# Conv-capsule and attention kernel on one Trainium2 core: the attention loop's body holds four units in place of two

## The chip, the core and the metric

The program runs on one core of a Trainium2 chip. A core has a matrix engine (TensorE, PE in the profile, with its weight loads shown apart as PEld), a vector engine (VectorE, DVE), a scalar engine (ScalarE, ACT), GpSimd (POOL) and SyncE (SP), which here only issues DMA transfers. Each engine has a sequencer of its own that walks through that engine's instructions; engines meet through semaphores. The metric is device time in microseconds (us) for the whole program. Time before: 13452.97 us, the median of three runs (13446.22 to 13472.08).

## The reference

Input x is 16 x 32 x 64 x 64, float32. Layer 0 adds a convolutional capsule layer with three routing rounds to x, layer 1 adds an attention block over 3x3 patches. The change touches only the attention of layer 1:

```
t = patches of the group-normed x          # per sample 4096 tokens x 288
z = _ln2(t)                                # normed over the whole sample
qkv = (z @ Wr.T) @ Wqkv.T                  # 8 heads of 18, tokens in 4 chunks of 1024
attn = softmax(q @ k.T * 18 ** -0.5)       # 1024 x 1024 within a chunk and a head
t = t + concat_heads(attn @ v) @ Wp.T + bp
t = t + relu(_ln2(t) @ W1.T + b1) @ W2.T + b2
out = fold of t back to the image (overlapping patches summed)
```

## The kernel before

The program is five phases, one after the other, with a barrier between them: a group norm (`norm_phase`), the capsule routing (`routing_phase`), a second norm that also prepares the layer norm, attention (`attention_phase`), and the MLP with the fold (`fold_phase`). In the profiled execution the attention phase takes the time from about 4550 to 12680 us.

A unit of attention is one chunk of one sample: 16 samples x 4 chunks make 64 units, numbered 0 to 63, of 1024 tokens each. `unit(p, which)` is written once for each engine; p holds the unit's number n, its parity h (which of two buffers) and m = n // 2, each a Python number or, in the loop, an expression of the loop's register. `which` says which neighbours' work is done beside unit n: 0 is the unit itself, 1 the row maxima for the next unit, 2 the projections and the staging through DRAM for the one after, -1 the remains of the one before. In a unit TensorE goes through 32 steps of four pairs. A pair is one score matmul (L1325, `a_sc`) and one matmul for the maxima of the next unit (L1337, `a_mp`). VectorE reduces each `a_mp` (L1503), ScalarE takes the exponential of each `a_sc` (L1423, 128 of them in a unit), and TensorE multiplies these with the values (L1351, `a_po`). `TASKS` puts the remaining work of a unit (projection, transposes, output) at fixed steps; "qk" of step 6 (L1269) reads the window `a_zw` that SyncE loads at the unit's start (L1138).

SyncE's part of a unit is `unit` at L1188: wait for the values' matmuls and load the window for unit n+2 (L1192), store and reload the row maxima (L1194), load patches (L1198), store results, write q and k parts to DRAM and read them back as stacks (L1215 and L1223). The last of these, 12 transfers of 144 KB (L1161), are issued when the last score of the unit is made.

`run_units` (L980) writes the same sequence for all engines: units -2 to 1 in straight code, a loop (`engine.Fori`, one for each engine, with a compare and branch at the end of its body that L986 marks in the profile), then units 62 to 64 in straight code. The loop runs 30 times over two units, 2 to 61 in all. Between two units of one body no branch stands; the 30th branch of an engine isn't taken. There is no barrier in the loop: engines hold each other only by semaphores. Order within an engine is as written; no scheduler changes it.

Of the kernel before, what the change touches and what calls it, by code (L numbers as in the profile page):

```python
# [979 lines left out]
def run_units(engine, units, unit):  # L980


    for n, which in ((-2, (2,)), (-1, (1, 2)), (0, (0, 1, 2)), (1, (-1, 0, 1, 2))):
        unit(Pass(n, n % 2, n // 2), which)
    if units > 4:
        with engine.Fori(0, units // 2 - 2) as i:  # L986
            unit(Pass(2 * i + 2, 0, i + 1), (-1, 0, 1, 2))
            unit(Pass(2 * i + 3, 1, i + 1), (-1, 0, 1, 2))
    for n, which in ((units - 2, (-1, 0, 1)), (units - 1, (-1, 0)), (units, (-1,))):
        unit(Pass(n, n % 2, n // 2), which)  # L990

# [8 lines left out]
def attention_phase(nc, ctx, sems, halves, ln_halves, mixed, moments, w_r, w_qkv, w_p, consts):  # L1000
# [126 lines left out]
    def _(sp):  # L1127
# [60 lines left out]
        def unit(p, which):  # L1188
# [31 lines left out]
            if 2 in which:  # L1220
                if 0 in which:
                    sp.wait_ge(score_made.sem, score_made.at(p.n, QUAD * STEPS))
                load_stack(offset(p, 2), 1)  # L1223

        run_units(sp, units, unit)
        for stored in t1_stored:
            sp.wait_ge(stored.sem, stored.at(units, 0))
# [3 lines left out]
    @block.gpsimd  # L1231
    def _(pool):
        def unit(p, which):
            for t in sorted(TASKS):
                d, kind, k = TASKS[t]
                if d in which and kind == "qk":
                    n = offset(p, d).n
                    pool.wait_ge(second.sem, second.at(n, k + 1))
                    nc.gpsimd.tensor_tensor(piece(k, 2), left[:, k % 2, 0:width(k)], piece(k, 1),  # L1239
                                            ALU.subtract).then_inc(third.sem, 1)  # L1240

        run_units(pool, units, unit)

    @block.tensor
    def _(pe):
# [110 lines left out]
        def unit(p, which):  # L1356
            for t in range(STEPS):
# [9 lines left out]
                task(p, t, which)  # L1367

        run_units(pe, units, unit)

    @block.scalar
# [533 lines left out]
```

## Time and profile before

| | |
|---|---|
| median of three runs | 13452.97 us |
| profiled execution, its own time | 13459.34 us |
| its span, first to last instruction | 13457.6 us |
| mean granted TensorE clock | 0.969 |
| TensorE busy (matmul) | 12585.8 us, 94% |
| VectorE busy | 9717.1 us, 72% |
| ScalarE busy | 7873.1 us, 59% |
| GpSimd busy | 2684.5 us, 20% |

The span is the profiled execution's own time less the 1.7 us around it. Busy shares are of the whole span. Matmul ends are modelled, so TensorE reads busier than it is. An idle time that is put down to "issue" is one in which the engine waited for nothing that the profile shows. Register, branch and semaphore instructions aren't counted as busy; they carry a q behind the engine's name (ACTq). In the profile FUSED_REGOPS is what the program's order calls ISA, ALU_OP is REGISTER_ALU.

### The profile page before, as it was taken

What the parts mean: (1) busy time and instruction counts of PE and PEld (TensorE: products, weight loads), DVE (VectorE), ACT (ScalarE), POOL (GpSimd) and SP (SyncE); (2) the same over time, 40 slices, a digit from 0 to 9 for tenths busy, and PEclk for the clock granted to TensorE, in tenths of its full rate; (3) what the DMA queues carried; (4) which work ended last, traced back from release to release, by engine and by line L of the source; (5) the groups of instructions that cost most, each with busy time, mean ns of one, the idle gap of its engine ahead of it and who ended that gap; (6) DMA issues with size and microseconds to landing.
All of it is one profiled execution on the core that took longest, in us unless ns stands there. A gap on an engine that the chain in (4) does not pass through costs nothing. (4 is left out here: it accounts for less than half of the span.)

```text
span 13457.6 us, 258672 instructions
## 1 busy us (share of the span) xinstructions
PE 12585.8 (94%) x76348; PEld 5302.5 (39%) x76348; DVE 9717.1 (72%) x18034; ACT 7873.1 (59%) x14774; POOL 2684.5 (20%) x2692
## 2 busy tenths in 40 slices
PE   6999999999996599999999999999999999999899
PEld 3554454554443133333333333333333333333233
DVE  7888888888887577777777777777777777777411
ACT  4666666666665266666666666666666666666511
POOL 3444454444443000000000000000000000000144
PEclk9999999999998699999999999999999999999999
DMA  3101101011012432232332332232232232232354
GB/s 75 22 15 22 22 15 22 15 22 21 16 22 76 107 72 62 69 68 62 70 67 62 70 67 62 69 68 62 69 68 62 69 69 62 68 69 62 73 121 106
DMA packets 853449, 773.62 MB, mean 57 GB/s; under 512 B 587076, under 2 KB 621348, under 8 KB 840740
## 3 DMA queue, kind: packets, MB, share of 16 engines
q1 hardware_dynamic: 850468, 747.29, 24.6%
q8 instruction: 744, 12.19, 0.4%
q10 hardware_dynamic: 1536, 8.39, 0.3%
q14 instruction: 701, 5.74, 0.2%
HBM read 510.50 MB, written 244.96 MB: 56 GB/s over the span
## 5 line engine op out<-in xcount | busy, mean ns | idle before, releaser
L1503 DVE TENSOR_REDUCE a_big<-a_mp 128x1 f32<-128x512 f32 x8192 | 5230.6, 685 | 2109.0 <-PE a_mp L1337 1978.0
L1423 ACT ACTIVATE a_ex<-a_sc 128x512 f32<-128x512 f32 x8192 | 4430.5, 600 | 2227.1 <-PE a_sc L1325 1918.1
L1325 PE MATMUL a_sc<-a_qs,a_ks 111*128 111x512 bf16 x8192 | 3166.8, 388 | 227.0 <-ACT a_ex L1423 152.2
L1337 PE MATMUL a_mp<-a_ks,a_qs 108*128 108x512 bf16 x8192 | 3173.2, 388 | 32.6 <-DMA a_ks<-qk_parts 25.1
L849 DVE TENSOR_TENSOR r_prod<-r_pg,r_win 128x512 f32<-128x512 f32 x3584 | 2317.0, 682 | 528.3 <-PE r_pg L583 287.6
L1351 PE MATMUL a_po<-a_ex,a_va 128*32 128x512 f32 x16384 | 2208.3, 611 | 1.4 <-ACT a_oc L1429 0.7
L1325 PEld LDWEIGHTS a_sc<-a_qs,a_ks 111*128 111x128 bf16 x8192 | 802.2, 98 | 2750.6 <-ACT a_ex L1423 1902.3
L1239 POOL TENSOR_TENSOR a_pieces<-a_left,a_pieces 128x512 bf16<-128x512 f32 x256 | 295.5, 1154 | 7622.9 <-ACT a_pieces L1409 7622.9
L524 POOL TENSOR_TENSOR r_prod<-r_temp,r_win 128x512 f32<-128x512 f32 x1024 | 1215.1, 1207 | 1394.7 <-PE r_pl L632 594.0
L587 PE MATMUL r_pg<-r_ident,r_spread 128*128 128x128 f32 x9216 | 1194.9, 278 | 112.0 <-DVE r_prod L849 93.4
L587 PEld LDWEIGHTS r_pg<-r_ident,r_spread 128*128 128x128 f32 x9216 | 1004.0, 142 | 567.5 <-DVE r_prod L849 266.1
L1337 PEld LDWEIGHTS a_mp<-a_ks,a_qs 108*128 108x128 bf16 x8192 | 810.6, 99 | 888.0 <-DVE a_big L1503 192.2
L582 PE MATMUL r_pg<-r_stack,r_wv 96*128 96x512 bf16 x2304 | 895.7, 389 | 73.1 <-DVE r_prod L849 55.9
L807 ACT ACTIVATE r_spread<-r_low 128x2048 f32<-128x2048 f32 x512 | 952.0, 1916 | 0.0
L583 PE MATMUL r_pg<-r_stack,r_wv 128*128 128x512 bf16 x2304 | 891.1, 387 | 0.0
L1269 PE MATMUL a_pm<-a_zw,a_wc 96*128 96x512 f32 x1536 | 716.4, 603 | 15.2 <-DVE a_left L1473 13.9
L1351 PEld LDWEIGHTS a_po<-a_ex,a_va 128*32 128x32 f32 x16384 | 324.3, 108 | 849.4 <-ACT a_ex L1423 690.8
L629 PE MATMUL r_ps<-r_prod,r_ws 128*32 128x512 f32 x4096 | 551.4, 611 | 26.0 <-DVE r_prod L849 18.1
L1808 DVE TENSOR_TENSOR f_u<-f_pw,f_three 96x512 f32<-96x512 f32 x128 | 87.8, 686 | 652.9 <-PE f_pw L1677 652.9
L790 ACT COPY r_temp<-r_pg 128x512 f32<-128x512 f32 x1024 | 544.5, 583 | 20.6 <-ACT r_out_t L775 20.6
L632 PE MATMUL r_pl<-r_prod,r_pick 128*32 128x512 f32 x4096 | 549.3, 608 | 4.9 <-DVE r_prod L849 0.5
L582 PEld LDWEIGHTS r_pg<-r_stack,r_wv 96*128 96x128 bf16 x2304 | 226.7, 98 | 692.7 <-DVE r_prod L849 323.1
(192 smaller groups left out, 11673.6 us busy)
## 6 DMA issues: line engine op xcount, KB each, us to landing
a_qs<-qk_parts SPq DMA_DIRECT2D x768, 144.0 KB
a_ks<-qk_parts SPq DMA_DIRECT2D x768, 144.0 KB
qk_parts<-a_pieces SPq DMA_DIRECT2D x128, 768.0 KB, 4.9
f_t<-mixed SPq DMA_DIRECT2D x48, 1536.0 KB, 16.5
a_tw<-second SPq DMA_DIRECT2D x512, 128.0 KB, 3.1
mixed<-a_t SPq DMA_DIRECT2D x256, 256.0 KB, 2.1
r_win<-first SPq DMA_DIRECT2D x128, 280.5 KB, 5.3
a_zw<-layered SPq DMA_DIRECT2D x192, 144.0 KB, 11.4
```

The lines of the kernel that those rows point to most:

```text
L524: nc.gpsimd.tensor_tensor(prod[:, g, :].rearrange("p (a b) -> p a b", b=IMG), temp[:, rank, :].rearrange("p (a b) -> p a b", b=IMG), tap_a ...
L582: pe.matmul(bank[:, :], wv_0[0:96, w], stack[0:96, lane, :], start=True, stop=False)
L583: last = pe.matmul(bank[:, :], wv_12[:, w], stack[:, lane, :], start=False, stop=True)
L587: last = pe.transpose(bank[:, 128 * b:128 * b + 128], spread[:, lane, 16 * kk:16 * kk + 16, :].rearrange("p a b -> p (a b)"), ident[:, :])
L807: nc.scalar.activation(to[:, :, half, :], src[:, :, half].unsqueeze(3).to_broadcast([128, BLK, 64, CLEN]), ACT.Exp).then_inc(prob[r].sem, 1)
L849: nc.vector.tensor_tensor(prod[:, g, :].rearrange("p (a b) -> p a b", b=IMG), pg[use % RINGS][:, :].rearrange("p (a b) -> p a b", b=IMG), ...
L1269: last = pe.matmul(pm[:, :], wc[:, i, 128 * (k % WIDE):128 * (k % WIDE) + 128], zw[:, own.h, first:first + CHUNK], start=i == 0, stop=i == 2)
L1325: pe.matmul(sc[k % BANKS][:, :], ks[0:KROWS + NPART, p.h, head, 128 * kb:128 * kb + 128], qs[0:KROWS + NPART, p.h, head, CHUNK * qb:CHUNK ...
L1337: pe.matmul(mp[k % BANKS][:, :], qs[0:KROWS, p.h, head, 128 * q:128 * q + 128], ks[0:KROWS, p.h, head, CHUNK * half:CHUNK * half + CHUNK], ...
L1351: last = pe.matmul(po[32 * x:32 * x + 32, :], va[:, p.h, kb, QUAD * quad + x, :], ex[:, (QUAD * t + x) % RING, :], start=kb == 0, stop=kb ...
L1423: nc.scalar.activation(ex[:, k % RING, :], sc[k % BANKS][:, :], ACT.Exp, scale=scale).then_inc(exped.sem, 1)
L1503: nc.vector.tensor_reduce(big[:, x % 2, k // 2:k // 2 + 1], mp[k % BANKS][:, :], AX_X, ALU.max).then_inc(maxed.sem, 1)
```

## The change

The loop's body is written for four units; the loop runs 15 times. The units' numbers, their order and the code before and after the loop are as they were. Unit k of the body has parity k % 2 and m = 2i + 1 + k // 2, the values that it had.

```diff
     if units > 4:
-        with engine.Fori(0, units // 2 - 2) as i:
-            unit(Pass(2 * i + 2, 0, i + 1), (-1, 0, 1, 2))
-            unit(Pass(2 * i + 3, 1, i + 1), (-1, 0, 1, 2))
+        with engine.Fori(0, (units - 4) // 4) as i:
+            for k in range(4):
+                unit(Pass(4 * i + 2 + k, k % 2, 2 * i + 1 + k // 2), (-1, 0, 1, 2))
```

ScalarE's order at the end of the second unit of a body, before the change: its last exponentials, and the loop's branch.

```order
1510 L1420 REGISTER_ALU
1511 L1423 ACTIVATE a_ex<-a_sc 128x512
1512 L1420 REGISTER_ALU
1513 L1423 ACTIVATE a_ex<-a_sc 128x512
1514 L986 REGISTER_ALU
1515 L986 COMPARE_AND_BRANCH
```

The same place with the change:

```order
1510 L1420 REGISTER_ALU
1511 L1423 ACTIVATE a_ex<-a_sc 128x512
1512 L1420 REGISTER_ALU
1513 L1423 ACTIVATE a_ex<-a_sc 128x512
1514 L1420 ISA
1515 L1422 REGISTER_ALU
1516 L1423 ACTIVATE a_ex<-a_sc 128x512
```

The branch has gone from here (it now stands at row 2174), and the third unit's exponentials follow at once. ScalarE's body grows from 672 to 1331 rows, its head stays at row 845.

SyncE's order at the same place (`a_qs` and `a_ks` are the stacks, `a_zw` the window), before:

```order
437 L1161 DMA a_qs<-qk_parts 18x4x1024
438 L1161 DMA a_ks<-qk_parts 18x4x1024
439 L986 REGISTER_ALU
440 L986 COMPARE_AND_BRANCH
```

and with the change:

```order
437 L1161 DMA a_qs<-qk_parts 18x4x1024
438 L1161 DMA a_ks<-qk_parts 18x4x1024
439 L1191 ISA
440 L1138 ISA
441 L1138 DMA a_zw<-layered 32x18x64
442 L1138 ISA
```

The window load of the next unit follows without a branch; SyncE's branch stands at row 615, and its body has 363 rows where it had 188. On TensorE and VectorE the branch goes from the same place in the same way (rows 3306 and 2014 before, 4487 and 2634 now), on GpSimd the body grows from 22 to 42 rows.

## Rows read from the trace of the kernel before

**Rows 1.** The page: an engine's busy us, share of the span, instructions

```profile
PE 12585.8 (94%) x76348; PEld 5302.5 (39%) x76348; DVE 9717.1 (72%) x18034; ACT 7873.1 (59%) x14774; POOL 2684.5 (20%) x2692
```

**Rows 2.** Busy time by stretch; columns are in the first line

```profile
core 0: us, PE busy (x) PEld busy (x) DVE busy (x) ACT busy (x) POOL busy (x), PEclk, DMA share, GB/s
4650.00:5128.00 478.00, 477.65 (x2644) 180.95 (x2644) 365.21 (x651) 312.81 (x617) 21.15 (x20) 0.99 0.27 64
5142.00:5146.00 4.00, 3.21 (x9) 1.25 (x9) 1.71 (x3) 3.71 (x8) 0.00 (x0) 0.50 0.68 140
5146.00:5380.00 234.00, 233.96 (x1305) 89.44 (x1307) 175.91 (x314) 151.27 (x299) 10.58 (x10) 1.00 0.27 63
```

**Rows 3.** L986, whole run: operation, count; ns min/median/max; first and last start

```profile
L986 PEldq ALU_OP  x30: 32/32/32, 5129.1 to 12455.2; - x30
L986 PEldq COMPARE_BRANCH  x30: 83/3662/3930, 5129.2 to 12455.3; - x30
...
L986 ACTq COMPARE_BRANCH  x30: 40/45/59, 5130.5 to 12456.5; - x30
...
L986 DVEq COMPARE_BRANCH  x30: 55/63/74, 5132.3 to 12458.4; - x30
...
L986 PEldq MOVE  x1: 34/34/34, 4887.3 to 4887.3; - x1
```

**Rows 4.** L986, from 5128 to 5140 us: the first branch of each engine

```profile
L986 ACTq COMPARE_BRANCH  x1: 59/59/59, 5130.5 to 5130.5; - x1
...
L986 DVEq COMPARE_BRANCH  x1: 74/74/74, 5132.3 to 5132.3; - x1
...
L986 ACTq FUSED_REGOPS  x1: 73/73/73, 5134.4 to 5134.4; - x1
...
L986 SPq COMPARE_BRANCH  x1: 50/50/50, 5136.8 to 5136.8; - x1
L986 SPq FUSED_REGOPS  x1: 68/68/68, 5137.1 to 5137.1; - x1
L986 DVEq FUSED_REGOPS  x1: 85/85/85, 5138.0 to 5138.0; - x1
```

**Rows 5.** Timeline of ACT and PE, same boundary: start, us, instruction, [idle before <-releaser]

```profile
5142.14 2.07 ACT L1423 ACTIVATE a_ex<-a_sc 128x512 f32<-128x512 f32 x4 [11.13 <-issue]
...
5142.79 0.61 PE L1325 MATMUL a_sc<-a_qs,a_ks 111*128 111x512 bf16 x1 [6.08 <-ACT a_ex L1423]
```

**Rows 6.** Timeline of ACT, boundary inside a body

```profile
5263.32 1.68 ACT L1423 ACTIVATE a_ex<-a_sc 128x512 f32<-128x512 f32 x3 [0.76 <-PE a_sc L1325]
```

**Rows 7.** Timeline of ACT, 5890 to 5902, boundary with a branch

```profile
5899.97 2.06 ACT L1423 ACTIVATE a_ex<-a_sc 128x512 f32<-128x512 f32 x4 [8.97 <-issue]
```

**Rows 8.** Timeline of ACT, 11190 to 11202, boundary with a branch

```profile
11200.48 2.07 ACT L1423 ACTIVATE a_ex<-a_sc 128x512 f32<-128x512 f32 x4 [8.78 <-issue]
```

**Rows 9.** Timeline of ACT, 12213 to 12216, last branch that is taken

```profile
12214.38 2.06 ACT L1423 ACTIVATE a_ex<-a_sc 128x512 f32<-128x512 f32 x4 [10.16 <-issue]
```

**Rows 10.** L1423, whole run: what ended ACT's idle time; us, times

```profile
  issue: 308.0, 60
```

**Rows 11.** L317, the routing loop's branch, 744 to 760 us

```profile
L317 ACTq COMPARE_BRANCH  x1: 45/45/45, 752.5 to 752.5; - x1
...
L317 ACTq FUSED_REGOPS  x1: 59/59/59, 754.9 to 754.9; - x1
```

**Rows 12.** The window load L1138, 5137 to 5260 us

```profile
L1138 SPq DMA_DIRECT2D a_zw<-layered x3: 332/789/3787, 5137.4 to 5138.9; - x3
...
DMA to landing us min/median/max: 8.0/10.4/10.7
```

**Rows 13.** Its reader L1269, same stretch

```profile
L1269 PEld LDWEIGHTS a_pm<-a_zw,a_wc x24: 187/190/192, 5168.1 to 5192.9; 96*128 96x128 f32 x24
```

**Rows 14.** The page, DMA queues of instruction code: packets, MB, share

```profile
q8 instruction: 744, 12.19, 0.4%
...
q14 instruction: 701, 5.74, 0.2%
```

## The prediction

> **What bounds the kernel now.** I read the page's busy times first. TensorE is busy 94% of the span [rows 1], and in straight attention code all of it: 477.65 of 478.00 us between 4650 and 5128 [rows 2]. So inside a unit TensorE sets the pace, and this change gives TensorE no less to do: matmuls, exponentials, reductions and transfers are the same in number and order. What can move is the code between units, so I went to the loop's own line, L986.
>
> There the branch itself is seen. On ScalarE and VectorE it takes 45 and 63 ns, on TensorE 3662 ns in the median, and only 83 ns where it isn't taken (the minimum, the last of 30) [rows 3]. ScalarE's and VectorE's branches are short but what follows is not. At the first loop end ScalarE branches at 5130.5 and the body's first instruction runs at 5134.4, 3.9 us later; VectorE goes from 5132.3 to 5138.0, 5.7 us; SyncE from 5136.8 to 5137.1, 0.3 us [rows 4]. A sequencer that jumps back to a body it has long passed must get that code again, and waits for it; SyncE's short body was still at hand. The timeline then shows the whole price. ScalarE's first exponential comes at 5142.14, after 11.13 us idle with nothing that released it, and TensorE, which had got going, waits 6.08 us for ScalarE [rows 5]. ScalarE is therefore the engine whose restart ends last. Its head runs three instructions (front order: the head at row 845) and then waits a second time, 5134.4 to 5142.1, which I take for a second piece of code that has to come. After that TensorE runs at a granted clock of 0.50 for about 4 us, 1.2 GHz in place of 2.4, and is back at 1.00 in the next stretch [rows 2]; its matmul takes 0.61 us there [rows 5]. What it did before was to stand idle for 6 us.
>
> At a boundary inside a body nothing of this is seen: the exponential at 5263.32 starts after 0.76 us of an ordinary wait for its score, and the next unit's follow it without a gap [rows 6]. So one back branch costs some ten microseconds on the path, and I have 29 of them that are taken.
>
> **The change part by part.** Price of one taken branch, three ways. (a) Whole iterations: TensorE's branch goes from 5129.1 to 12455.2 in 29 iterations, 7326.1 / 29 = 252.6 us each; the first iteration, which is entered from straight code, takes 4887.3 to 5129.1, 241.8 us [rows 3]. The difference is 10.8 us, and holds the low clock too. (b) The last taken branch: ScalarE stands 10.16 us [rows 9] and its loop ends at 12456.5 [rows 3], 242.1 us after it restarts at 12214.4; with the half microsecond from a branch to the next exponential that is 242.6, so 252.6 - 242.6 = 10.0 us. (c) All the idle time of ScalarE before L1423 that nothing released is 308.0 us in 60 times [rows 10]; even if all of it were these 29, it is 10.6 each. I take 10.3, the middle of (a) and (b).
>
> Removed: 30 iterations have 29 taken branches, 15 have 14. 15 x 10.3 = 154.5 us. The idle times are not equal: of the 29, seven are short ones of 8.2 to 9.0 us, the first at 5899.97 with 8.97, the last at 11200.48 with 8.78 [rows 7, 8], the others 10.2 to 11.9. From unit 12 on the short ones come before every eighth unit (12, 20, 28, ...). The new loop ends stand before units 6, 10, 14, ... 58, so if the short ones belong to the unit, six of the seven are among the removed, and the removed 15 are worth 0.5 us less each than the mean, 147 us in all. If they belong to the count of loop ends, nothing is lost. I can't tell which, and take half: 154.5 - 4 = 150 us.
>
> Kept: the 14 branches that remain. Nothing before the loop changes and the body's head is the same on each engine, so the jump lands at the same place of the code, and ScalarE should wait twice as now. The branch's distance grows, but on TensorE, VectorE and ScalarE the head was already gone. I cost this at zero change, with bounds 2.2 us either way per branch (the difference between a short and a long idle time), 31 us over 14.
>
> New boundaries: 15 places where the third unit follows the second without a branch. The order rows show ScalarE with one ISA and one register operation where branch and head stood. A boundary of that parity is seen in the straight code before the loop, which runs four units without a branch at 0.99 of the clock [rows 2]. Cost zero; the cover is that TensorE has matmuls queued.
>
> SyncE: its body grows from 188 to 363 rows. Now it does not wait at its branch. ScalarE's routing loop of 459 rows (131 to 590 in the order) does, from 752.5 to 754.9, 2.4 us [rows 11]. 363 lies between the two, nearer to the one that waits, so I expect SyncE to wait 2.4 us or more at the 14 branches. Queued behind is the window load L1138, then the row maxima's store. Now the last window transfer starts at 5138.9 and lands at the latest 10.7 us later, 5149.6 [rows 12]; its reader on TensorE starts at 5168.1 [rows 13]. 18.5 us of slack hide 2.4 us, and also the 11.6 us that ScalarE's restart takes (5130.5 to 5142.1). The store after it is for scores half a unit, 60 us, later. What SyncE can cost is its fetch standing in the way of ScalarE's second one: between nothing and 3.9 us, ScalarE's first wait [rows 4], on 14 branches, 0 to 55 us; or a gain, since the window load then leaves the queues free while ScalarE's code comes, up to the 2.2 us above. The nearest row is the loop end as it is, so I take zero and keep both ends.
>
> GpSimd's body grows from 22 to 42 rows; it works 10 instructions in two units and waits for others. Zero. The fold loop behind lies at another place of the code; its bodies are short, and I cost it at zero.
>
> Sum against the profiled execution: span 13457.6 - 150 = 13308, its own time 13459.3 - 150 = 13309. The median of the runs is 6.4 us below the profiled one, so the forecast is 13453 - 150 = 13303 us, 1.1% less.
>
> **Where the Trainium skill is weighed.** The trace shows 3662 ns for TensorE's branch and 10 us for the whole stop. The Trainium skill, Advanced Engine Details and Errata, Control Flow Timing, gives about 108 ns for a compare-and-branch; by that figure alone 15 of them would be worth 1.6 us and the change would do nothing. For the branch on ScalarE and VectorE the trace is below that figure (45 and 63 ns), for what follows it is not. The Trainium skill, Runtime: NRT & Kernel Launch, Instruction fetch mechanics, says that a taken branch to code outside the small window of instruction memory stalls for a fetch, and that straight code is fetched ahead. By this rule rows 4 and 6 are what one should see, and the sum is the one above. The same section gives the window as 512 instructions on the engines other than TensorE. By that rule SyncE's body would still fit and its branch stay cheap; ScalarE's routing loop, with 459 rows, speaks against it, and the sum is the same either way.
>
> **The rivals.** First, the kept stops get longer. Each of 14 is 3.9 us dearer because SyncE now fetches as well: 150 - 55 = 95 us gained, 13358 us. For it: fetches and data use the same DMA engines, and the stack transfers are issued right there. Against: SyncE branches 6 us after ScalarE, when ScalarE's second fetch should be under way.
>
> Second, the stop moves instead of going: a branch costs only a fetch, and the pace inside a unit takes back what was won, as VectorE or SyncE's transfers are late at the new boundaries. That is no change, 13453 us. By the Trainium skill's figure for a branch (Advanced Engine Details and Errata, Control Flow Timing) it would come out there too, at 13451. For it: nothing in TensorE's work gets less. Against: the boundaries inside a body show 0.76 us [rows 6], and the units after them keep step.
>
> Third, slower: SyncE's restart makes the window late. Its load would reach TensorE after the reader's place at step 6, and TensorE would stand, once in four units. It decides from 18.5 us of SyncE waiting; to eat all 150 us it needs another 10.7 us on each of 14, that is 29 us. At 32 us it would be 14 x 13.5 = 189 lost against 150 won, 13492 us. The longest restart in the trace is 11.6 us, three such in a row would do it. I give it 1 in 50.
>
> Fourth, the kept stops get shorter: the window load comes later and ScalarE's second piece sooner, all 14 like the short ones, 150 + 31 = 181 us won, 13272 us.
>
> **How the numbers follow.** Forecast 72%, within 13285 to 13325 (price 10.0 to 10.8, 150 to 162, less up to 8, and some 1 us per kept branch). Longer stops 14%, shorter stops 8%, no change 4%, slower 2%. Range 13270 to 13350: below it takes in the fourth case, above most of the first; about 1 in 10 is left out. A measurement of this kernel can tell 0.2%, some 27 us, from no change: faster 0.94, same 0.04, slower 0.02.
>
> **What would show it.** Right: 15 branches per engine on L986, TensorE's again near 3.7 us; 14 iterations of about 242 + 242.5 + 10.3 = 495 us from branch to branch; ScalarE's idle time before L1423 put down to issue falls from 308 to about 150 us; at old loop ends such as 5142 a normal boundary; the mean clock a little up from 0.969. SyncE's branch then a wait of 2 us or more and no wait of TensorE's L1269 for a DMA. The packets of instruction code should fall on q8, from 744 [rows 14], as code fetched beyond the branch and thrown away is fetched half as often; on q14 less, as SyncE's come in. Wrong: iterations of over 500 us, a wait of TensorE for the window, or new idle times of 1 us and more at the branchless boundaries.

## The result: 13278 us, 174 us less

| | before | with the change |
|---|---|---|
| median | 13452.5 us (4 runs) | 13278.3 us (4 runs, 13273.5 to 13281.0) |
| ratio, 95% interval | | 0.9868 (0.9851 to 0.9885) |
| profiled execution, its span | 13457.6 us | 13271.7 us |
| mean granted TensorE clock | 0.969 | 0.975 |

The kernel is 174 us faster, where 150 was forecast; the time lies inside the range of 13270 to 13350. It is 7 us below the likeliest case's own range, 13285 to 13325, and nearer to the fourth rival's 13272 than to the forecast of 13303. Two of the executions below ran at a far lower granted clock, one of the kernel before (18863.5 us) and one of e9 (23326.3 us); the ratios, and the median of e9, leave them out.

### The profile page after: what moved, and what is told of

Read it like the earlier page. It is cut to its first block and busy times, and to the rows that moved or that the text cites. A ratio compares the mean times of both kernels' runs of the same rounds, so it can differ in the third digit from the quotient of the medians.

```text
span 13271.7 us, 257906 instructions
## 1 busy us (share of the span) xinstructions
PE 12514.4 (94%) x76092; PEld 5293.0 (40%) x76348; DVE 9713.2 (73%) x18034; ACT 7869.7 (59%) x14774; POOL 2683.8 (20%) x2692
## 5 line engine op out<-in xcount | busy, mean ns | idle before, releaser
L1423 ACT ACTIVATE a_ex<-a_sc 128x512 f32<-128x512 f32 x8192 | 4428.9, 601 | 2057.7 <-PE a_sc L1325 1919.6
L849 DVE TENSOR_TENSOR r_prod<-r_pg,r_win 128x512 f32<-128x512 f32 x3584 | 2319.6, 683 | 520.2 <-PE r_pg L583 263.0
L583 PE MATMUL r_pg<-r_stack,r_wv 128*128 128x512 bf16 x2048 | 785.5, 384 | 0.0
L1269 PE MATMUL a_pm<-a_zw,a_wc 96*128 96x512 f32 x1536 | 710.2, 598 | 15.0 <-DVE a_left L1473 13.3
```

What stands on the lines that cost most here:

```text
L583: last = pe.matmul(bank[:, :], wv_12[:, w], stack[:, lane, :], start=False, stop=True)
L849: nc.vector.tensor_tensor(prod[:, g, :].rearrange("p (a b) -> p a b", b=IMG), pg[use % RINGS][:, :].rearrange("p (a b) -> p a b", b=IMG), ...
L1269: last = pe.matmul(pm[:, :], wc[:, i, 128 * (k % WIDE):128 * (k % WIDE) + 128], zw[:, own.h, first:first + CHUNK], start=i == 0, stop=i == 2)
L1423: nc.scalar.activation(ex[:, k % RING, :], sc[k % BANKS][:, :], ACT.Exp, scale=scale).then_inc(exped.sem, 1)
```

## The profile after

The page's first line with the change; it answers to [rows 1].

```profile
PE 12514.4 (94%) x76092; PEld 5293.0 (40%) x76348; DVE 9713.2 (73%) x18034; ACT 7869.7 (59%) x14774; POOL 2683.8 (20%) x2692
```

TensorE's work is the same. The 71 us by which its busy time fell are not a measure of the gain, since this trace lacks 256 records of a routing matmul (L583, 2048 in place of 2304). The rows of L986 over the whole run (operation, count, ns min/median/max, first and last start) answer to [rows 3]:

```profile
L986 PEldq ALU_OP  x15: 32/32/32, 5355.8 to 12268.6; - x15
L986 PEldq COMPARE_BRANCH  x15: 83/3665/3882, 5355.9 to 12268.7; - x15
...
L986 ACTq COMPARE_BRANCH  x15: 40/45/59, 5357.2 to 12269.9; - x15
...
L986 DVEq COMPARE_BRANCH  x15: 55/63/74, 5359.1 to 12271.8; - x15
...
L986 PEldq MOVE  x1: 34/34/34, 4872.2 to 4872.2; - x1
```

Each engine has 15 branches, and TensorE's costs what it did, 3665 ns in the median. From branch to branch TensorE takes (12268.6 - 5355.8) / 14 = 493.8 us for four units. The first iteration, entered from straight code and now four units long, takes 5355.8 - 4872.2 = 483.6 us, 120.9 for a unit. The difference is 10.2 us for a stop, by which I mean all that one taken back branch costs, on all engines together. At the first loop end, which now comes after unit 5, the same line reads (it answers to [rows 4]):

```profile
L986 ACTq COMPARE_BRANCH  x1: 59/59/59, 5357.2 to 5357.2; - x1
...
L986 DVEq COMPARE_BRANCH  x1: 74/74/74, 5359.1 to 5359.1; - x1
...
L986 ACTq FUSED_REGOPS  x1: 74/74/74, 5360.9 to 5360.9; - x1
...
L986 SPq COMPARE_BRANCH  x1: 50/50/50, 5361.6 to 5361.6; - x1
L986 DVEq FUSED_REGOPS  x1: 85/85/85, 5365.1 to 5365.1; - x1
L986 SPq FUSED_REGOPS  x1: 68/68/68, 5369.4 to 5369.4; - x1
```

ScalarE has its head after 3.7 us, VectorE after 6.0. SyncE, which waited 0.3 us before, now waits 7.8. The timeline at that loop end (start, us, instruction, idle time before it and what ended it) has the stop that [rows 5] had, ScalarE last again:

```profile
5368.30 2.06 ACT L1423 ACTIVATE a_ex<-a_sc 128x512 f32<-128x512 f32 x4 [10.56 <-issue]
...
5368.95 0.61 PE L1325 MATMUL a_sc<-a_qs,a_ks 111*128 111x512 bf16 x1 [6.50 <-ACT a_ex L1423]
```

At the place where the loop ended before and doesn't now, in front of unit 4, ScalarE's row has turned into that of a boundary inside a body, as [rows 6]:

```profile
5115.41 1.68 ACT L1423 ACTIVATE a_ex<-a_sc 128x512 f32<-128x512 f32 x3 [0.76 <-PE a_sc L1325]
```

Here is L1423 over the whole run. Its first row counts all exponentials with the start of the first and the last; the second is the idle time that nothing released, 308.0 us in [rows 10]:

```profile
L1423 ACT ACTIVATE a_ex<-a_sc x8192: 587/597/654, 4636.4 to 12462.9; 128x512 f32<-128x512 f32 x200
...
  issue: 137.1, 30
```

The same first row of the kernel before:

```profile
L1423 ACT ACTIVATE a_ex<-a_sc x8192: 587/598/647, 4651.4 to 12649.5; 128x512 f32<-128x512 f32 x200
```

From the first to the last exponential the attention took 12649.5 - 4651.4 = 7998.1 us before and takes 12462.9 - 4636.4 = 7826.5 us now, 171.6 less. This length leaves out the phases ahead of the attention, which neither change nor experiments up to the ninth touch and whose time moved by up to 20 us between profiled executions. I use it below to price a stop. The window load behind SyncE's stop, which answers to [rows 12], and its reader, as [rows 13]:

```profile
L1138 SPq DMA_DIRECT2D a_zw<-layered x3: 337/353/522, 5369.7 to 5370.9; - x3
...
DMA to landing us min/median/max: 3.6/3.7/4.0
```

```profile
L1269 PEld LDWEIGHTS a_pm<-a_zw,a_wc x24: 187/190/192, 5393.2 to 5418.0; 96*128 96x128 f32 x24
```

The load is issued at 5370.9, lands within 4.0 us, and its reader starts at 5393.2, so 18 us of slack are left, as before. The packets of instruction code (queue: packets, MB, share), as [rows 14]:

```profile
q8 instruction: 729, 11.94, 0.4%
...
q14 instruction: 715, 5.85, 0.2%
```

## The experiments

My theory (A) is that each taken back branch costs a reload of code on three engines, and straight code costs nothing; the main rival (B) is that the gain came from elsewhere. Theories C to G, each with its rival, ask what sets the length of a stop. Each kernel was timed against the kernel before. The two-unit kernel is the kernel before, the four-unit kernel is the one with the change. The stop is worked out as (length - 7682.0) / taken branches, where 7682.0 us is the length of the straight kernel e1, from first to last exponential.

| kernel | taken branches | median us | ratio (95%) | length us | one stop us |
|---|---|---|---|---|---|
| before, two units | 29 | 13452.5 | 1 | 7998.1 | 10.90 |
| the change, four units | 14 | 13278.3 | 0.9868 (0.9851 to 0.9885) | 7826.5 | 10.32 |
| e1 straight | 0 | 13139.2 | 0.9777 (0.9760 to 0.9793) | 7682.0 | - |
| e2 two units, ScalarE's head moved | 29 | 13300.7 | 0.9900 (0.9884 to 0.9917) | 7841.3 | 5.49 |
| e3 two units, stack transfers later | 29 | 13248.6 | 0.9859 (0.9842 to 0.9875) | 7795.1 | 3.90 |
| e4 two units, window load later | 29 | 13422.7 | 0.9989 (0.9979 to 0.9999) | 7976.9 | 10.17 |
| e5 e2 and e3 together | 29 | 13254.8 | 0.9855 (0.9839 to 0.9872) | 7795.0 | 3.90 |
| e6 four units, ScalarE's head moved | 14 | 13217.4 | 0.9828 (0.9812 to 0.9844) | 7755.7 | 5.26 |
| e7 six units | 9 | 13230.7 | 0.9836 (0.9820 to 0.9853) | 7780.9 | 10.99 |
| e8 two units, SyncE's body longer | 29 | 13435.1 | 0.9989 (0.9979 to 0.9999) | 7973.9 | 10.07 |
| e9 six units, window load later | 9 | 13223.5 | 0.9828 (0.9809 to 0.9848) | 7776.1 | 10.46 |
| e10 attention and routing straight | 0 | 12991.8 | 0.9659 (0.9643 to 0.9675) | - | - |

The kernel before measured 13437 us beside e1 to e4, 13448 beside e5 to e7, 13444 beside e8 and e9, and 13451 beside e10, so compare by ratio.

Each length comes from one profiled execution. It can be had twice for straight code: e10, whose attention is that of e1, has 12180.3 - 4497.9 = 7682.4 us, 0.4 us more than e1. The single stops of one execution differ more: from branch to branch of TensorE they come to 8.1 to 13.0 us in the kernel before, 8.4 to 11.3 with the change and 9.5 to 12.1 in e7. The standard error of the mean stop (how far chance alone may well move it) is 0.2 us over 29 of them and 0.3 us over 14 or 9, so a difference of 0.6 us between two means says little by itself.

### e1: no loop at all

```diff
-        with engine.Fori(0, (units - 4) // 4) as i:
-            for k in range(4):
-                unit(Pass(4 * i + 2 + k, k % 2, 2 * i + 1 + k // 2), (-1, 0, 1, 2))
+        for n in range(2, units - 2):
+            unit(Pass(n, n % 2, n // 2), (-1, 0, 1, 2))
```

> All 60 units of the loop in straight code, no loop and no branch on any engine. Theory A (each taken back branch costs a reload of code, 10.88 us in the two-unit kernel and 10.29 us in the four-unit one, and straight code costs nothing): 14 stops of 10.29 us go, 144 us below the four-unit kernel, 13134 us; every unit takes 120.87 us, and ScalarE's idle time put down to issue before L1423 nearly vanishes. Rival B (the gain of the change came from something else than the branches, or a program with 30 times the loop's code loses by fetching what branches save): 13278 us or more, with idle times strewn over the units.

Measured: 13139.2 us. It is 298 us below the kernel before beside it, and the length is 144.5 us below the four-unit kernel's, against 144 expected. The exponentials' row and what ended their idle time; no time is left for "issue":

```profile
L1422 ACT ACTIVATE a_ex<-a_sc x8192: 585/599/647, 4640.6 to 12322.6; 128x512 f32<-128x512 f32 x200
...
  PE a_sc L1324: 1919.7, 2803
```

TensorE in the 60 units that had been the loop (columns in the first line):

```profile
core 0: us, PE busy (x) PEld busy (x) DVE busy (x) ACT busy (x) POOL busy (x), PEclk, DMA share, GB/s
4881.00:12133.00 7252.00, 7249.88 (x40442) 2751.33 (x40441) 5531.90 (x9901) 4752.02 (x9421) 317.63 (x300) 1.00 0.30 69
```

It is busy 7249.88 of 7252.00 us and keeps its clock at 1.00. So the branches were the whole difference, and straight code of this length is fetched without any cost that can be seen. Straight code also has fewer instructions (220357 records in place of 257906), as the units' numbers are no longer worked out from the loop's register. That isn't where the time went: a unit inside the loop took 120.9 us as well, as long as no branch stood in it. The packets of instruction code fell on both queues:

```profile
q8 instruction: 647, 10.60, 0.3%
...
q14 instruction: 462, 3.78, 0.1%
```

Theory A holds, rival B falls. This version beats both kernels.

### e2: ScalarE's head somewhere else

```diff
-        act.wait_ge(prepared, 1)
+        for _ in range(17):
+            act.wait_ge(prepared, 1)
```

The 16 waits more, all already met, make 8 instructions more (258680 records in place of 258672).

> The two-unit kernel with 16 more waits that are already met, on ScalarE alone, ahead of its loop: its loop head lies 8 instructions later in the code. Theory A (ScalarE waits twice because its head lies two instructions ahead of the edge of a piece of code): its second wait (7.7 us) goes, VectorE's restart, 7.6 us after ScalarE's branch, is the last one, so the stop shrinks from 10.9 to about 7 us; 29 x 4 = 116 us gained, 13336 us. Rival C (the time is that of the transfers, however the pieces are cut, because the second piece is needed soon anyway): 13452 us, and a wait of like length some instructions later.

Measured: 13300.7 us, 136 below the kernel before beside it, and 5.49 us for a stop. That is more than theory A had promised (116 us, a stop of about 7): VectorE's late restart holds the others up less than I had assumed.

```profile
L1424 ACT ACTIVATE a_ex<-a_sc x8192: 586/598/648, 4632.9 to 12474.2; 128x512 f32<-128x512 f32 x200
```

At one of the loop ends, L986 and then ScalarE's timeline:

```profile
L986 ACTq COMPARE_BRANCH  x1: 45/45/45, 5608.6 to 5608.6; - x1
...
L986 DVEq COMPARE_BRANCH  x1: 63/63/63, 5610.5 to 5610.5; - x1
...
L986 ACTq FUSED_REGOPS  x1: 68/68/68, 5611.4 to 5611.4; - x1
...
L986 DVEq FUSED_REGOPS  x1: 85/85/85, 5615.5 to 5615.5; - x1
```

```profile
5612.20 0.60 ACT L1424 ACTIVATE a_ex<-a_sc 128x512 f32<-128x512 f32 x1 [3.04 <-PE a_sc L1325]
...
5616.65 0.60 ACT L1424 ACTIVATE a_ex<-a_sc 128x512 f32<-128x512 f32 x1 [2.23 <-PE a_sc L1325]
```

ScalarE has its head 2.8 us after the branch and goes on at once. It waits only for scores now, at 5612.20 and again at 5616.65. VectorE's head comes at 5615.5 and was not touched. The second wait of 7.7 us has gone and did not return some instructions later, so it hung on where the head lay in the code, as theory A has it. Rival C falls. That it was the edge of a fetched piece is inferred from its going away when the head moved.

### e3: the stack transfers off the loop's end

```diff
             if 0 in which:
                 load_max(p, 1)
+                if -1 in which and 1 in which:
+                    sp.wait_ge(score_made.sem, score_made.at(p.n, 0))
+                    load_stack(p.to(1), 1)
...
             if 2 in which:
-                if 0 in which:
-                    sp.wait_ge(score_made.sem, score_made.at(p.n, QUAD * STEPS))
-                load_stack(offset(p, 2), 1)
+                if 0 not in which:
+                    load_stack(offset(p, 2), 1)
```

In the same version the wait for half of a unit's scores stands ahead of the wait for the stored parts in place of behind it; both come before the same load. SyncE also comes to its branch and its window load earlier, by some 4 us before TensorE's branch, so e3 takes all of SyncE's transfers away from the loop's end and not the stacks alone.

> The two-unit kernel with SyncE's 12 stack transfers of the unit's end issued in the next unit, behind the store of the row maxima, so that none of them is under way at the loop's end. Theory D (the code comes slowly, 3.9 us and then 7.7 us, because these 1.7 MB fill the DMA engines; in the routing loop, without such a burst, ScalarE restarts in 2.4 us): both waits shrink to about 2.5 us, the stop to 5 or 6 us; 29 x 5 = 145 us gained, 13307 us. Rival E (a code fetch takes what it takes): 13452 us, stop still 10.9.

Measured: 13248.6 us, 188 below the kernel before beside it, and 3.90 us for a stop. The exponentials' row, and a loop end:

```profile
L1425 ACT ACTIVATE a_ex<-a_sc x8192: 586/599/653, 4640.5 to 12435.6; 128x512 f32<-128x512 f32 x200
```

```profile
L986 PEldq COMPARE_BRANCH  x1: 3927/3927/3927, 5608.8 to 5608.8; - x1
...
L986 ACTq COMPARE_BRANCH  x1: 45/45/45, 5610.1 to 5610.1; - x1
...
L986 DVEq COMPARE_BRANCH  x1: 63/63/63, 5612.0 to 5612.0; - x1
L986 ACTq FUSED_REGOPS  x1: 68/68/68, 5612.6 to 5612.6; - x1
L986 PEldq FUSED_REGOPS  x1: 68/68/68, 5612.8 to 5612.8; - x1
L986 DVEq FUSED_REGOPS  x1: 85/85/85, 5614.9 to 5614.9; - x1
```

```profile
5615.53 1.57 ACT L1425 ACTIVATE a_ex<-a_sc 128x512 f32<-128x512 f32 x3 [4.90 <-PE a_sc L1327]
```

ScalarE's head comes after 2.5 us (3.1 in the mean of the 29 before), VectorE's after 2.9 (4.9). ScalarE goes on at 5615.53, 5.4 us after its branch, in place of 10.9 in the mean of the 29 before. In the 6 us from ScalarE's branch on (5610 to 5616 us) the DMA engines are busy for a share of 0.04 and move 11 GB/s; at the same loop end of the kernel before (5638 to 5644) it is 0.53 and 118 GB/s. So ScalarE's and VectorE's fetches were slow because data transfers were under way; for the most part these were the stacks, as the window load alone is worth little (e4). TensorE's fetch was not: its branch takes 3750 ns in the median here and 3662 before, where it came 1.2 us ahead of the first stack transfer (5129.2 and 5130.4 us). Theory D holds for two engines and rival E falls. With the loop at two units this one move is worth as much as the change under study.

### e4: the window load behind the row maxima

```diff
             if 2 in which:
-                if 0 in which:
-                    sp.wait_ge(v_made.sem, v_made.at(p.n, 3))
-                load_window(offset(p, 2))
+                if 0 not in which:
+                    load_window(offset(p, 2))
             if 0 in which:
                 load_max(p, 1)
+                if 2 in which:
+                    sp.wait_ge(v_made.sem, v_made.at(p.n, 3))
+                    load_window(offset(p, 2))
```

> The two-unit kernel with SyncE's window load behind the reload of the row maxima in place of ahead of it, so that it is issued when ScalarE has restarted. Theory F (the stops of the four-unit kernel are 0.6 us shorter, 10.29 in place of 10.88, because SyncE now waits 7.8 us at its branch and its window load no longer stands beside ScalarE's second fetch): 29 x 0.6 = 17 us gained, 13435 us. Rival: they are shorter by the position of the loop ends or by chance of the pieces' timing: 13452 us.

Measured: 13422.7 us, 14 below, the interval of the ratio just excludes 1. The length is the better measure: 7976.9 us, 21 less, 0.73 us for a stop. Theory F had 17 us and 0.6; with standard errors of 0.2 us on either mean this is for it, but not by much.

```profile
L1425 ACT ACTIVATE a_ex<-a_sc x8192: 587/597/654, 4642.5 to 12619.4; 128x512 f32<-128x512 f32 x200
```

### e5: e2 and e3 together

> Both edits of the two-unit kernel at once: the stack transfers off the loop's end, and ScalarE's head 8 instructions later. With the transfers moved alone a stop costs 3.9 us, which is also what TensorE's own restart takes (3.98 us from branch to work). Theory G (the stop is now TensorE's own reload, ScalarE's two waits lie beside it): nothing more is gained, 13249 us within 10, 3.9 us for a stop. Rival (ScalarE's second wait, 5.3 us after its branch, is still the last): its restart falls to 3 us and 29 x 2 = 58 us are gained, 13190 us.

Measured: 13254.8 us, and the same length as e3 to 0.1 us.

```profile
L1426 ACT ACTIVATE a_ex<-a_sc x8192: 587/598/647, 4643.7 to 12438.7; 128x512 f32<-128x512 f32 x200
```

So with the transfers gone ScalarE's second wait costs nothing, and theory G's figure, 3.9 us for a stop against 3.97 us from TensorE's branch to its first work in the mean of this run's 29, fits. It isn't shown further than that: no run made TensorE's own reload shorter.

### e6: ScalarE's head moved in the four-unit kernel

The edit is that of e2.

> The four-unit kernel with ScalarE's head 8 instructions later. In the two-unit kernel this took a stop from 10.9 to 5.5 us. Theory A: the same at 14 stops, 10.3 to 5.5, 67 us, 13211 us against 13278. Rival (SyncE, which now waits 7.2 us at its branch, or VectorE is late next): less than 20 us gained, 13260 or more.

Measured: 13217.4 us, 7755.7 us in length, 70.8 less than with four units alone (67 expected).

```profile
L1424 ACT ACTIVATE a_ex<-a_sc x8192: 587/597/648, 4638.2 to 12393.9; 128x512 f32<-128x512 f32 x200
```

### e7: six units in an iteration

```diff
-        with engine.Fori(0, (units - 4) // 4) as i:
-            for k in range(4):
-                unit(Pass(4 * i + 2 + k, k % 2, 2 * i + 1 + k // 2), (-1, 0, 1, 2))
+        with engine.Fori(0, (units - 4) // 6) as i:
+            for k in range(6):
+                unit(Pass(6 * i + 2 + k, k % 2, 3 * i + 1 + k // 2), (-1, 0, 1, 2))
```

> Six units in an iteration, 10 iterations, 9 taken branches, 5 fewer than with four units. Theory A: 5 x 10.3 = 51 us, 13227 us. Rival (a longer body makes each stop dearer): more than 13240 us, and stops above 10.3 us.

Measured: 13230.7 us. The length fell by 45.6 us, against 51 expected.

```profile
L1423 ACT ACTIVATE a_ex<-a_sc x8192: 587/598/647, 4641.3 to 12422.2; 128x512 f32<-128x512 f32 x200
```

The median lies between theory A's 13227 and the 13240 above which the rival has it. A stop costs 10.99 us here, more than with four units (as the rival has it) and as much as with two, though SyncE waits at its branch as it does with four. That spoke against theory F, and e8 and e9 were made for it.

### e8: SyncE's body as long as with four units

```diff
                 a = offset(p, 2)
+                if -1 in which:
+                    for _ in range(220):
+                        sp.wait_ge(fixed, 16)
                 sp.wait_ge(third.sem, third.at(a.n, OUTS))
```

> The two-unit kernel with 110 instructions more in each unit on SyncE (220 waits that are already met, where it waits for GpSimd anyway), so that its body is as long as with four units and it should reload it at its branch. Theory F (a SyncE that waits at its branch, and so loads the window later, shortens each stop by 0.6 us): SyncE waits 7 us at its branch, a stop costs 10.2 us in place of 10.9, 13430 us. Rival: the third engine that fetches makes stops dearer, 10.9 or more, 13447 us or above; or they stay at 10.9 and the difference between the two- and four-unit kernels lies elsewhere.

Measured: 13435.1 us, 9 below, and 10.07 us for a stop, 0.83 less than before. SyncE now waits 7.4 us at the first loop end, with nothing changed but the length of its body:

```profile
L986 SPq COMPARE_BRANCH  x1: 45/45/45, 5137.5 to 5137.5; - x1
L986 SPq FUSED_REGOPS  x1: 68/68/68, 5144.9 to 5144.9; - x1
```

```profile
L1426 ACT ACTIVATE a_ex<-a_sc x8192: 587/597/654, 4652.2 to 12626.1; 128x512 f32<-128x512 f32 x200
```

So a SyncE that has to wait for its own code seems to make the others' stop a little shorter, 0.8 us with a standard error of 0.3, and theory F holds for two units. That it does so by moving the window load is argued, from e4.

### e9: six units, window load later

> The six-unit kernel, whose stops cost 11.0 us though SyncE waits 7.5 us at its branch, with the window load behind the reload of the row maxima. Theory F (SyncE's own wait already moves the window load out of the way): nothing is left to gain, 13231 us, 11.0 us a stop. Rival (the window load still falls on ScalarE's second fetch): 9 x 0.7 = 6 us less in the attention loop, 13225 us.

Measured: 13223.5 us, and 4.8 us less length than e7, 0.53 for a stop. This is what the rival has (6 us), but nine stops of one execution don't tell 0.5 us from nothing, so it stays open whether SyncE's wait alone had done it.

```profile
L1425 ACT ACTIVATE a_ex<-a_sc x8192: 587/597/648, 4644.8 to 12420.9; 128x512 f32<-128x512 f32 x200
```

Why the nine stops of e7 are dearer than the 14 of the four-unit kernel stays open. Single stops vary by some 2 us, and the difference, 0.7 us with a standard error of 0.4, may be chance.

### e10: the routing loop straight as well

```diff
-        with engine.Fori(0, passes // 2 - 1) as i:
-            for s in range(SLOTS):
-                slot(Pass(2 * i + 1, 1, i), s, heavy=True, which=(-1, 0, 1))
-            for s in range(SLOTS):
-                slot(Pass(2 * i + 2, 0, i + 1), s, heavy=True, which=(-1, 0, 1))
+        for n in range(1, passes - 1):
+            for s in range(SLOTS):
+                slot(Pass(n, n % 2, n // 2), s, heavy=True, which=(-1, 0, 1))
```

> The straight attention kernel, and the routing phase's loop (15 iterations of two passes, 14 taken branches) written straight too. Theory A: what a stop costs there is set by TensorE's reload, 3.7 to 3.9 us, since ScalarE and VectorE restart in 2.4 to 5 us and no stack transfers are under way: 14 x 3.8 = 53 us below the attention-only version, 13086 us. Rival (the routing's engines have queued work that covers the reload): under 15 us gained, 13125 or more.

Measured: 12991.8 us, 147 us below e1 (159 by the ratios) where 53 was expected. VectorE's products (same code, two lines apart) in e1 and then in e10, with the first and last start at the end:

```profile
L849 DVE TENSOR_TENSOR r_prod<-r_pg,r_win x3584: 674/681/693, 115.8 to 4238.7; 128x512 f32<-128x512 f32 x200
```

```profile
L847 DVE TENSOR_TENSOR r_prod<-r_pg,r_win x3584: 671/681/694, 114.7 to 4094.8; 128x512 f32<-128x512 f32 x200
```

From first to last they took 4122.9 us with the loop and 3980.1 without, so (4122.9 - 3980.1) / 14 = 10.2 us for a stop, where I had 3.8. The size was missed by a factor of 2.7: I had looked at each engine's first restart only. The trace of e1 shows a second one. After the loop end at which VectorE branches at 750.49, it waits, works for about a microsecond and waits again, with nothing that released it:

```profile
754.07 0.69 DVE L849 TENSOR_TENSOR r_prod<-r_pg,r_win 128x512 f32<-128x512 f32 x1 [3.50 <-PE r_pg L583]
...
759.77 1.89 DVE L849 TENSOR_TENSOR r_prod<-r_pg,r_win 128x512 f32<-128x512 f32 x3 [4.59 <-issue]
```

At all 14 taken branches VectorE has such a second wait of 3.2 to 6.0 us, which ends 8.0 to 11.4 us after its branch, 9.7 in the mean. The idle time that nothing released (us, times), before L849 in e1 and then before L847 in e10, where it is gone:

```profile
  issue: 56.7, 12
```

```profile
  issue: 0.3, 1
```

So here VectorE looks like ScalarE in the attention loop, with a head that comes in two pieces. No run moved VectorE's head, so this cause isn't shown.

## Why the prediction was right, and what was off in size

**The bound and the mechanism** held. TensorE sets the pace inside a unit, a taken back branch costs a reload on three engines, and ScalarE's second wait ends last. e1 takes the branches away and gains 144.5 us over the four-unit kernel where 144 was expected; e2 and e3 take away ScalarE's second wait and the transfers beside it, and gain 157 and 203 us by length where 116 and 145 were expected, both more than their theories had.

**The price of a taken branch** was set at 10.3 us, between 10.0 and 10.8; it is 10.9. Way (a) had it. Way (b) looked only at ScalarE's idle time and the unit behind a single stop. This put 15 x 10.9 = 163.5 in place of 154.5, so 9 of the missing 22 us by length.

**The correction for short stops**, -4 us, and **the kept stops**, costed at no change with 2.2 us either way, can be counted in two ways. By the mean stop, the removed ones were worth 163.5 us without a correction, and the kept ones are 0.6 us cheaper, 14 x 0.6 = 8 us. The sum is then 163.5 + 8.1 = 171.6 us, which is what the length gives. Stop by stop it looks different. ScalarE's idle time before L1423 was 9.9 us in the mean of the 15 ends that went and 10.9 in the mean of the 14 that stayed, and is 9.6 in the mean of these 14 now. By these idle times, and this is an estimate, the removed stops were worth some 156 us (163.5 less 7.5, the whole of the correction of which I took half), and the kept ones got some 16 us cheaper. The short ones didn't stay with their units either: before unit 18 ScalarE had waited 10.9 us and now waits 8.8. So the kept stops were a term that was set too low: they gave 8 to 16 of the missing 22 us, the fourth rival at a quarter to a half of its 31. By e4 and e8 its mechanism is likely: SyncE comes late and so does its window load.

**SyncE's body** does miss, as its 363 rows near the routing loop's 459 suggested. It waits 7.8 us rather than 2.4, and hidden all the same: the window's reader keeps its 18 us. The Trainium skill's window of 512 instructions for this engine (Runtime: NRT & Kernel Launch, Instruction fetch mechanics) would, taken as a bare number, have let it fit. The trace and e8, where the engine's body alone was made longer, say that it is loaded again. The same section's rule on taken branches and straight code agrees with e1: no stop is left in 7252 us. The 108 ns for a branch (the Trainium skill, Advanced Engine Details and Errata, Control Flow Timing) is no price for a loop's end, which is 10.9 us here.

**The rivals.** Longer stops (13358): the third engine's fetches did not stand in ScalarE's way; in e8 the stops got shorter with them. No change (13453): refuted by e1; the pace inside a unit took nothing back, the 60 straight units take 7252 / 60 = 120.9 us each. Slower (13492): the window was never late. Its "longest restart in the trace", 11.6 us, was that of the first loop end; ScalarE's longest is 12.4, before unit 58. Shorter stops (13272): right in sign, a quarter to a half in size.

**The signs.** The 15 branches, the stop near 10.3, the 0.76 us at the old loop end and the clock at 0.975 came as said. An iteration was forecast at 495 us and took 493.8. ScalarE's idle time for "issue" fell to 137.1, a little below the 150 named. q8 fell from 744 to 729 only, less than "code fetched half as often" had made me expect, and q14 rose from 701 to 715 where I had it fall: with SyncE's pieces the sum hardly moved.

**Two readings** in the prediction were off without moving the forecast. The range of the likeliest case, added up from its own terms, reaches down to 13453 - 162 - 14 = 13277 and not to 13285; the measured 13278 lies in it. And the low clock lasts longer than 4 us, which was only the width of the stretch in [rows 2]. On both sides of that stretch it reads

```profile
5134.00:5142.00 8.00, 2.71 (x12) 0.31 (x10) 1.89 (x3) 0.00 (x0) 0.00 (x0) 0.53 0.72 140
5146.00:5148.00 2.00, 2.00 (x10) 0.20 (x8) 1.06 (x2) 0.60 (x1) 0.00 (x0) 0.50 0.66 123
```

with the clock as the third number from the end: it fell soon after 5134, so ahead of the 6 us in which TensorE waited for ScalarE and behind the 2.6 us in which it had waited for its own code. The price of a stop holds all of this, as it was taken from whole iterations.

## What to carry to other kernels

Price a loop's end by the branch's own line on each engine and by the first work after it, and count the engine that restarts last, not the branch. Where a body is long, write more of it straight, up to the whole loop. Where it must loop, keep bursts of transfers away from the loop's end, and see whether an engine's head is fetched in two steps: at two units the first is worth 188 us here and the second 136, without a longer program; both together give no more than the first (e5). Look beyond the first instructions of the body for the second wait, on every engine (e10).

## What the runs showed of the hardware

- Code and data compete. With 12 transfers of 144 KB issued at the loop's end VectorE's head came after 4.9 us in the mean; with the same transfers issued 12 us behind TensorE's branch (e3) it came after 3.0. TensorE's own reload, which starts ahead of them, was no slower with them: 3.66 us in the median, and 3.75 in e3.
- Where a loop's head lies in an engine's code is worth time: 8 instructions ahead of the loop took a stop from 10.9 to 5.5 us, with ScalarE's code alone touched (e2).
- SyncE reloads a body of 363 rows (7.2 us from branch to head in the mean) and does not reload one of 188 (0.3 us). In e8, with its longer body, the others' stop was 0.8 us shorter.
- A stop of TensorE is paid twice: at the first loop end its granted clock is 0.50, 1.2 GHz, until 5148 us, and its score matmuls take 0.63 us in place of 0.38; in straight code over 7252 us the clock stays at 1.00, 2.4 GHz (e1).
- The routing loop's stop costs 10.2 us. Each engine's first restart there comes within about 5 us, but VectorE waits a second time, until 9.7 us after its branch in the mean.
